# Picked tokens of batches 0 to 23 gathered within the last batch's body, value projections ahead of the head projections

## What is computed

```python
x = x + xattn(layernorm(x), ctx)
...
q = rms_norm(x @ q_w + q_b) * norm_q_w
out = attention(q, k_txt, v_txt) + attention(q, k_img, v_img)
x = x + out @ o_w + o_b
```

```python
scores = layernorm(x) @ w_router
idx = sort(top_k(scores, 14))
h = rms_norm(sel, ln1_w)
q, k, v = h @ wq + bq, h @ wk + bk, h @ wv + bv
q, k = rope(q), rope(k)
x1 = sel + causal_attention(q, k, v) @ wo
mlp = (silu(h2 @ w_gate) * (h2 @ w_up)) @ w_down
gated = sigmoid(score) * (x1 + mlp) + (1 - sigmoid(score)) * sel
output = layernorm(x).at[idx].set(gated)
```

## Time and profile before

| | us |
|---|---|
| median of 3 runs (lowest, highest) | 1652.77 (1651.08, 1653.58) |
| the profiled execution | 1652.05 |
| its span in the profile | 1650.3 |
| PE busy (share of the span) | 1569.6 (95%) |
| VectorE, ScalarE, GpSimd busy | 1188.0, 706.1, 700.7 |
| mean granted TensorE clock (share of 2.4 GHz) | 0.979 |

### The profile page before, as it was taken

How to read it: one execution, slowest core, us unless ns; L and a number is a source line. 1 busy time by engine, 2 the same in 40 slices (tenths; PEclk the granted TensorE clock), 3 DMA queues, 4 the chain that set the end, 5 groups by cost and what they waited for, 6 DMA issues and landing times.

```text
span 1650.3 us, 42268 instructions
## 1 busy us (share of the span) xinstructions
PE 1569.6 (95%) x16777; PEld 1219.0 (74%) x16777; DVE 1188.0 (72%) x1871; ACT 706.1 (43%) x1448; POOL 700.7 (42%) x775
## 2 busy tenths in 40 slices
PE   6999999999999999999999999999983999998997
PEld 5776777777777777777777777777762887777896
DVE  5754788787887878878788788887764675444775
ACT  5763444434444344444444444444431214555331
POOL 6761443444434444344443444434423770113552
PEclk9999999999999999999999999999986899999998
DMA  6842111121111211112111121111126205010000
GB/s 188 248 126 70 48 51 50 46 75 59 52 46 46 76 58 52 46 46 76 58 52 46 49 75 56 52 46 54 56 104 224 90 1 205 26 52 26 1 1 23
DMA packets 66151, 113.71 MB, mean 69 GB/s; under 512 B 21376, under 2 KB 36064, under 8 KB 64560
## 3 DMA queue, kind: packets, MB, share of 16 engines
q1 hardware_dynamic: 65264, 110.20, 21.0%
q0 software_dynamic: 832, 2.75, 0.7%
...
## 4 chain that ended last, share of the span: by engine, by line
PE 88%; ACT 5%; DVE 3%; issue 1%; POOL 1%; DMA 1%; SPq 0%; DVEq 0%; ACTq 0%; POOLq 0%
PE ps L1294 21%; PE ps L1295 18%; PE ps L1296 18%; PE ps L1424 7%; PE ps L1399 7%; PE ps L1372 3%; PE ps L1346 3%; PE ps L1578 2%; ACT prob L731 2%; PE ps L1402 2%; PE ps L1559 2%; PE ps L1570 1%; ACT prob L729 1%; PE ps L1328 1%; PE ps L1379 1%
## 5 line engine op out<-in xcount | busy, mean ns | idle before, releaser
L485 POOL TENSOR_TENSOR ctx_lo<-ctx_raw,ctx_hi 128x472 fp32r<-128x472 f32 x64 | 115.2, 1823 | 310.6 <-ACT ctx_hi L672 310.6
L522 POOL TENSOR_TENSOR prob_img<-prob 128x448 f32<-128x448 f32 x128 | 160.5, 1254 | 192.7 <-ACT prob L731 192.7
L1001 DVE RECIPROCAL rec<-ps 128x224 f32<-128x224 f32 x128 | 199.0, 1555 | 7.1 <-PE ps L1424 3.4
L729 ACT ACTIVATE prob<-ps 119x448 f32<-119x448 f32 x128 | 69.7, 545 | 212.9 <-PE ps L1402 212.9
L990 DVE TENSOR_REDUCE top<-ps 112x4 f32<-112x1028 f32 x128 | 156.2, 1220 | 0.0
L1399 PEld LDWEIGHTS ps<-q_all,k_all 32*128 32x128 f32 (+1 forms) x3072 | 121.6, 186 | 45.9 <-issue 32.0
L1399 PE MATMUL ps<-q_all,k_all 32*128 32x112 f32 (+1 forms) x3072 | 148.0, 300 | 6.2 <-ACT prob L731 6.2
L705 ACT ACTIVATE sq_junk<-proj 128x513 bf16<-128x513 f32 (+1 forms) x96 | 61.1, 637 | 172.7 <-DVE proj L969 172.7
L989 DVE TENSOR_REDUCE top<-ps 112x4 f32<-112x472 f32 x128 | 83.0, 649 | 66.3 <-PE ps L1372 66.3
L731 ACT ACTIVATE prob<-ps 128x896 f32<-128x896 f32 x128 | 117.0, 914 | 0.0
L995 DVE SCALAR_TENSOR_TENSOR prob_img<-prob,ones_last,prob_img 23x448 f32<-23x448 f32 x128 | 87.5, 684 | 40.0 <-POOL prob_img L522 37.0
...
## 6 DMA issues: line engine op xcount, KB each, us to landing
...
xh_dram<-xh SPq DMA_DIRECT2D x32, 448.0 KB, 3.1
...
ring<-in_wq_dram SPq DMA_DIRECT2D x1, 4096.0 KB, 14.1
```

The source lines that it names most:

```text
L485: nc.gpsimd.tensor_tensor(ctx_lo[:, :, cols], ctx_raw[:, :, cols], ctx_hi[:, :, cols].bitcast(F32), ALU.subtract).then_inc(ctx_lo_done, 1)
L522: nc.gpsimd.tensor_tensor(prob_img[:, g % 2], prob[:, g % 2, 1, :], prob[:, g % 2, 2, :], ALU.add).then_inc(img_summed, 1)
L1001: nc.vector.reciprocal(rec[:], bank[:, 2:4]).then_inc(norm_step, 1)
```

## The change

The last body becomes a function of its own on each engine (`last`). In it the rows of batches 0 to 23 are chosen, their token numbers made, three of the four gathers issued (`gather`, the source cut to these batches' rows), squared (now on ScalarE), scaled (ScalarE), transposed and split. wv is loaded first in that body, wq and wk behind the store of batch 30. The root is a power on GpSimd (`token_roots`), without ScalarE's table. The output projection of batch 31 is cut in four (`output_part`), each part behind its group. After it PE makes value tiles for the three quarters (6 of 8), between which the links of the last quarter's chain stand; tiles 6 and 7 and then the heads follow. `wv_hi` and `head_hi` lie in another weight buffer, and wo comes in two halves. The router gates move from the value stage into the attention loop, and so do, later, the products that keep the tokens. Small tables and constants are loaded or made in the prologue.

```diff
+EARLY = NC - 1
+EARLY_B = EARLY * BPC
+VALUE_TILES = [(half, c) for half in range(2) for c in range(EARLY)] + [(half, EARLY) for half in range(2)]
...
-        wv_hi = ring_lo[0][:, 0:2 * FF].rearrange("p (c n) -> p c n", c=KC)
+        wv_hi = ring_lo[2][:, 0:2 * FF].rearrange("p (c n) -> p c n", c=KC)
+        head_hi = ring_lo[2][:, 2 * FF:3 * FF].rearrange("p (e c n) -> p e c n", e=4, c=KC)
...
+            def last(i, p):
+                sp.wait_ge(b1_full, value_slot(i, 1)[3] + 1)
+                sp.dma_start(wv, t["wv"].rearrange("(c p) n -> p c n", p=P)).then_inc(ring_loaded[1], 16)
+                sp.wait_ge(scaled, 3 * i + 3)
+                sp.dma_start(bv_row[:], t["bv"].partition_broadcast(L)).then_inc(fvec_loaded, 16)
+                store(p)
+                sp.wait_ge(xh_stored, 16 * i)
+                sp.dma_start(xh[:, 0], t["x"][bass.ds(i, 1)].rearrange("o t d -> t (o d)")).then_inc(xres_loaded, 16)
+                sp.dma_start(wq, t["wq"].rearrange("(c p) n -> p c n", p=P)).then_inc(ring_loaded[0], 16)
+                sp.wait_ge(ring_loaded[1], 16)
+                sp.dma_start(wk, t["wk"].rearrange("(c p) n -> p c n", p=P)).then_inc(ring_loaded[1], 16)
...
+            sp.dma_start(wo[:, 0:FH // 2], wo_rows[:, 0:FH // 2]).then_inc(ring_loaded[2], 16)
+            sp.wait_ge(head_full, FH)
             sp.dma_start(w_gate, t["w_gate"].rearrange("(c p) n -> p c n", p=P)).then_inc(ring_loaded[0], 16)
+            sp.wait_ge(head_full, FH + FKV)
+            sp.wait_ge(ring_loaded[2], 16)
+            sp.dma_start(wo[:, FH // 2:FH], wo_rows[:, FH // 2:FH]).then_inc(ring_loaded[2], 16)
             sp.dma_start(w_up, t["w_up"].rearrange("(c p) n -> p c n", p=P)).then_inc(ring_loaded[1], 16)
...
+            def gather(c):
+                nc.gpsimd.indirect_dma_start(xh_sel[:, c].rearrange("l a d -> l (a d)"), None, xh_dram[0:EARLY_B * L] if c < EARLY else xh_dram,
+                                             bass.IndirectOffsetOnAxis(ap=tok[:, c:c + 1], axis=0)).then_inc(gathered[c], 16)
+            def token_roots(cols, turn):
+                pool.wait_ge(sums_ready, cols.stop)
+                nc.gpsimd.tensor_scalar(sums[:, cols], sums[:, cols], 1.0 / D, RMS_EPS, ALU.mult, ALU.add).then_inc(root_ready, 1)
+                pool.wait_ge(root_ready, turn)
+                nc.gpsimd.tensor_tensor(rstd[:, cols], sums[:, cols], neg_half[0:L].to_broadcast([L, cols.stop - cols.start]), ALU.pow).then_inc(rstd_ready, 1)
+            def value_weights_lo(half, part):
+                pool.wait_ge(w_hi_done, half + 1)
+                at = (slice(None), slice(2 * part, 2 * part + 2), slice(512 * half, 512 * half + 512))
+                made = nc.gpsimd.tensor_tensor(wv_lo[at], wv[at], wv_hi[at].bitcast(F32), ALU.subtract)
+                if part:
+                    made.then_inc(w_lo_done, 1)
+            def last(i, p):
+                normalise_h(p)
+                output(p)
+                pool.wait_ge(tok_ready, 1)
+                pool.wait_ge(xh_stored, 16 * EARLY_B)
+                pool.wait_ge(scaled, 3 * i + 3)
+                pool.wait_ge(k_tail_done, i + 1)
+                gather(0)
+                sum_image(i, 0)
+                gather(1)
+                gather(2)
+                value_weights_lo(0, 0)
+                sum_image(i, 1)
+                value_weights_lo(0, 1)
+                sum_image(i, 2)
+                token_roots(slice(0, EARLY), 1)
+                sum_image(i, 3)
+                residual(i)
+                value_weights_lo(1, 0)
+                value_weights_lo(1, 1)
+            over_batches(pool, pre, body, last)
...
+            weights_lo(0)
+            pool.wait_ge(tok_ready, 2)
             pool.wait_ge(xh_stored, 16 * B)
-            for c in range(NC):
-                nc.gpsimd.indirect_dma_start(xh_sel[:, c].rearrange("l a d -> l (a d)"), None, xh_dram,
-                                             bass.IndirectOffsetOnAxis(ap=tok[:, c:c + 1], axis=0)).then_inc(gathered[c], 16)
+            gather(EARLY)
+            weights_lo(1)
+            token_roots(slice(EARLY, NC), 2)
+            weights_lo(2)
+            weights_lo(3)
...
+            def token_squares(c):
+                act.wait_ge(gathered[c], 16)
+                if c:
+                    act.wait_ge(sums_ready, c)
+                nc.scalar.activation(tok_junk[:], xh_sel[:, c, 1], ACT.Square, accum_out=sums[:, c:c + 1]).then_inc(sums_ready, 1)
+            def hT_early(kc):
+                act.wait_ge(hT_full, kc + 1)
+                at = FH + FKV + kc
+                nc.scalar.activation(hT_hi[:, kc, 0:EARLY * L], ps[:, 2 + kc, 0:EARLY * L], ACT.Copy, scale=fvec[:, at:at + 1]).then_inc(hT_hi_done, 1)
+            def last(i, p):
+                value_image(i, 1)
+                o_hi(p)
+                value_text(i)
+                turn_top(i, 0)
+                turn_top(i, 1)
+                exps(i, 0)
+                value_weights_hi(0)
+                exps(i, 1)
+                value_weights_hi(1)
+                token_squares(0)
+                token_squares(1)
+                exps(i, 2)
+                o_hi_part(i, 0)
+                token_squares(2)
+                exps(i, 3)
+                act.wait_ge(rstd_ready, 1)
+                for c in range(EARLY):
+                    nc.scalar.activation(normed[:, c], xh_sel[:, c, 1], ACT.Copy, scale=rstd[:, c:c + 1]).then_inc(normed_ready, 1)
+                o_hi_part(i, 1)
+                act.wait_ge(fvec_loaded, 16)
+                hT_early(0)
+                o_hi_part(i, 2)
+                for kc in range(1, KC):
+                    hT_early(kc)
+                o_hi_part(i, 3)
+            over_batches(act, pre, body, last)
...
+            def last(i, p):
+                group_max(i, 0)
+                dve.wait_ge(topk_loaded, 16 * 3)
+                choose(slice(0, EARLY_B), 1)
+                o_rest(p)
+                group_max(i, 1)
+                add_residual(p)
+                group_max(i, 2)
+                place(slice(0, EARLY_B), 1)
+                ln2(p)
+                group_max(i, 3)
+                tokens(slice(0, EARLY), 1)
+                score(p)
+                add_tail(i, 0)
+                ranks(p)
+                normalise(i, 0)
+                add_tail(i, 1)
+                normalise(i, 1)
+                o_rest_part(i, 0)
+                add_tail(i, 2)
+                add_tail(i, 3)
+                normalise(i, 2)
+                o_rest_part(i, 1)
+                normalise(i, 3)
+                o_rest_part(i, 2)
+                o_rest_part(i, 3)
+                dve.wait_ge(fvec_loaded, 16)
+                hT_rest(0)
+                hT_rest(1)
...
+            add_value_bias(0)
+            choose(slice(EARLY_B, B), 2)
+            add_value_bias(1)
+            place(slice(EARLY_B, B), 2)
+            tokens(slice(EARLY, NC), 2)
+            add_value_bias(2)
+            dve.wait_ge(gathered[EARLY], 16)
+            nc.vector.scalar_tensor_tensor(normed_last[:], xh_sel[:, EARLY, 1], 1.0, xh_sel[:, EARLY, 1], ALU.mult, ALU.mult,
+                                           accum_out=sums[:, EARLY:NC]).then_inc(sums_ready, 1)
+            add_value_bias(3)
+            dve.wait_ge(rstd_ready, 2)
+            nc.vector.tensor_scalar(normed_last[:], xh_sel[:, EARLY, 1], rstd[:, EARLY:NC], None, ALU.mult).then_inc(normed_ready, 1)
+            add_value_bias(4)
...
+            def last(i, p):
+                scores(i, 0)
+                values(i, 2)
+                scores(i, 1)
+                output(p)
+                pe.wait_ge(b0_done, 4 * i + 4)
+                count_before(slice(0, EARLY_B), 1)
+                scores(i, 2)
+                pe.wait_ge(pv_done, 4 * i)
+                turn_top(i, 0)
+                scores(i, 3)
+                find_tokens(range(EARLY), 1)
+                turn_top(i, 1)
+                scores_T(i, 0)
+                scores_T(i, 1)
+                pe.wait_ge(topT_ready, 2 * i + 2)
+                turn_score(p)
+                weighted_values(i, 0, None)
+                scores_T(i, 2)
+                pe.wait_ge(rank_done, i)
+                weighted_values(i, 1, None)
+                scores_T(i, 3)
+                weighted_values(i, 2, None)
+                output_part(i, 0)
+                weighted_values(i, 3, None)
+                pe.wait_ge(exp_done, 8 * i + 8)
+                pe.wait_ge(normed_ready, EARLY)
+                for kc in range(KC):
+                    for c in range(EARLY):
+                        made = nc.tensor.transpose(ps[:, 2 + kc, c * L:(c + 1) * L], normed[:, c, kc * P:(kc + 1) * P], ident[0:L, 0:L])
+                    made.then_inc(hT_full, 1)
+                for g in range(1, KC):
+                    output_part(i, g)
+            over_batches(pe, pre, body, last)
+            def value_tile(m, chunks=range(KC)):
+                half, c = VALUE_TILES[m]
```

(33 more changed lines are left out.)

431 lines of the change are left out of this document (193 added, 238 removed).

## The result

| | before | changed kernel |
|---|---|---|
| median of the runs | 1653.17 us | 1638.77 us |
| ratio to before, 95% interval | | 0.9912 [0.99, 0.9925] |
| profiled execution | 1652.05 us | 1640.35 us |
| its span | 1650.3 us | 1638.6 us |

Faster, by about 14 us (0.9%) where 21.7 were forecast. The time lies in the range (1625 to 1641), near its upper end. The profiled execution shows 11.7 us of gain. A second measurement of the same kernel, later, gave 1636.21 us (0.9895 [0.988, 0.991]).

What follows compares the result with a forecast made beforehand. It took one serial chain from batch 31's attention to head 0 as the bound, with 22 us of value projections behind. First exponential 22.7 us earlier less 1.0 gave 21.7: 1630.3 profiled, 1631.0 us median; range 1625 to 1641.

Steps and rivals of the forecast that it cites:

- D: Rival: PE's clock stays at half until heads and values are done; net 55 us slower, 1708; chance 0.01.
- E: Rival: early tokens late or a shared buffer holds value tiles until the last gather; only 1 to 2 us gained; chance 0.02.
- B: Rival: gathers come as before, gather 1 at 1239, the tie falls to PE's side, nothing lost at the seam; 1627; chance 0.15.
- C: Rival: last quarter's chain is the longer by far, a later bias addition holding the next link 4 us; 1635; chance 0.12.
- Step 1: Choice of the first three quarters in batch 31's body: first exponential's end moves from 1228.94 to 1229.9, +1.0 us.
- Step 2: Early gathers under the weight load: gather 1 takes 9.4 us and lands at 1241.0, bounds 1239 and 1250.
- Rival A: Gathers wait behind the weights: gather 1 at 1250, batch 31 behind it 9 us later; 12.7 gained, 1640; chance 0.18.
- Step 3: Rest of batch 31: last exponential ends at 1246.7, statistics 10.2 us later at 1256.9, 2.1 later than before.
- Step 4: Value tiles against the last quarter's chain, between batch 31 and heads: nearly tie at 1283.0 and 1284.7; heads start about 1284.0.
- Step 5: The heads: 24 at 2.47 us each, 59.3 us, to 1343.3.
- Step 6: Seam from heads to attention: 3.7 us, first exponential at 1347.0, 22.7 us earlier than before.
- Step 7: Attention and later: moved gate and token products, wo halves and PE's idle seam cost 1.0 us, bounds 0 and 2.

Runs made afterwards that it cites:

- the low parts moved: Changed kernel with GpSimd's two second-half value-weight low parts moved from behind batch 31's residual to ahead of the third image sum: 1631.34 us.
- the last kernel: Changed kernel with wq/wk loads after early gathers, low parts on VectorE (second half late), residual held, two score blocks ahead of heads 22 and 23: 1621.35 us.
- one input: Changed kernel with GpSimd's second-half low parts made by one-input instructions (weights times zero), leaving those low parts out of the output: 1631.58 us.

## Why the prediction was right and wrong

*Direction and mechanism: right.* The value tiles fill the last chunk's chain, PE works nearly without a break from 1264, and the run with the values put back behind the heads gives the whole gain back. Rivals D and E fell, and so did B and C: gather 1 was used at 1242.26, not 1239, and PE waited 0.86 us for the last quarter's tokens, not 4.

*Step 1: near, and not really tested.* First exponentials end at 1229.29 (1229.9 forecast), but that mark moved by 3 us between profiles of kernels that are the same up to there.

*Step 2: right within 1.3 us.* Gather 1 was used at 1242.26 (1241.0), 11.5 us behind its issue where I took 9.4, between the bounds. With the loads held back it took 5.4, so the load doubled it. By the Trainium skill ("DMA: Bandwidth & Descriptors", Queues, rings and completion order), an engine takes turns between queue rows packet by packet; by that rule, the trace agrees. Rival A's time, 1640, came nearly true in the profiled execution, but not by its mechanism: gather 1 was not at 1250.

*Step 3: wrong, and this is the step that failed.* Statistics of batch 31 were forecast for 1256.9 and end at 1265.68. Of the 8.8 us, 1.3 are the gather's; 5.6 are the fourth add_tail (6.29 in place of 0.68). Of the other 1.9, 0.5 lie ahead of the last exponential's end. The rest lies in the output products and splits: from the fourth add_tail's end to the statistics' end it took 9.65 us here, at a clock of 0.67 (1250 to 1260), and 8.39 with the low parts moved, at 1.00; but 9.10 in the last kernel, also at 1.00, so the clock alone doesn't explain it. The step said that GpSimd's low parts "lie inside waits". They do, as GpSimd's time. What I did not ask is what they do to VectorE while they run. The step priced them at nothing inside the waits, and at up to 3 us if the gathers came at once; with gather 1 at 5.4 us, PE waited 5.04 us for VectorE's side of it. Nor did the forecast see that they were cheap in the old place for a reason: GpSimd's two-input low parts of 4.65 us stood beside head reads the earlier trace rows, which take one operand from PSUM (ps). The trace of before does hold a hint: GpSimd's last image sum of batch 31 took 1.47 us, starting while VectorE's third add_tail ran, where the other three took 1.13. With the fault removed in either way (moved, or one input), the time is 1631.3 and 1631.6, against 1631.0 forecast; part of that agreement is chance, since gather and seam each cost more than forecast, and the one-input run leaves work out.

*Step 4: better than forecast.* Value tiles start at 1263.68, 2.0 us ahead of the statistics' end. From the statistics' end to the heads' start it took 24.9 us, where the forecast had 27.1 (1256.9 to 1284.0). The last gather, alone on the DMA engines, was used 4.4 us behind its issue (1274.23 to 1278.66), where I took 7.3 from four gathers in a row, and it was issued 8.6 us behind the statistics, not 10.6. Square, root and scaling took 4.4 us in place of 2.8, since the scaling, too, was long beside GpSimd (2.75 us, shown in the last section). PE stood idle for only 0.57 and 0.86 us from the first value tile to the heads, so its own work and the chain did nearly tie. Heads start at 1290.54.

*Step 5: right.* 2.48 us a head.

*Step 6: right on its own.* 3.3 us from the last head's read (1350.27) to the first exponential (3.7). It comes 6.6 us late because of step 3 (8.8), less what step 4 gave back (2.2).

*Step 7: mis-sized.* Forecast 1.0, bounds 0 to 2; measured 4.45 behind the first exponential: 2.9 to the root of sums (144.6 us, 141.8 before) and 1.6 behind that. The prediction's own sign of being wrong, an attention longer by over 2 us, came true. The low clock is some 2 us of it, as the two pairs of windows above show. The rest of the attention's loss and the 1.6 us of the tail, which varied from 137.6 to 141.1 us over kernels that are the same there, stay open. The upper bound of 2 us would have been the better choice for the clock's part. By the Trainium skill ("TensorE: Matmul & The Clock Gate", HAM oscillation), a gap throttles the clock and the next burst starts cold. By that rule the first profile of the changed kernel agrees (0.50 behind 2.17 us of idling); that of the low parts moved (1.00 behind the same 2.17 us) doesn't.

The sum: 6.6 late at the first exponential and 3.45 behind it make the 10.0 us between the forecast gain of 21.7 and the 11.7 of the profiled execution. By the medians 14.4 us were gained, 7.3 short. That the time lies in the range is luck in part: its upper end was set by rival A's slow gathers, and no rival named the blocking that took the 5.6 us.
